# A decoder layer on one core: context loads issued by ScalarE, two queues at the start, set-up products spread out, the last two bases kept on chip

## What is computed

```python
x = x + attention(layernorm(x))          # 16 heads of 32; q, k, v and output weights of 512x512
x = x + cross(ctx, ctx, layernorm(x))    # one head of 512 over 750 context rows
h = layernorm(x)
scores = (h @ Wq.T @ Wr.T) @ (keys @ Wr.T).T / sqrt(48) + mask     # 2048 keys
top, idx = top_k(scores, 8)
agg = sum(softmax(top) * values[idx])                  # gather of 8 rows of 512
var = log1p(variance(h));  u = 0.5 * var / (mean over the whole input of var + 1e-6)
gate = sigmoid(g * clip(u + 2.5 * sigmoid(learned(h)), 0, 5) + gb)
x = x + (h + gate * agg)
```

## Time and profile before, and how it is read

| what | before |
|---|---|
| median of 3 runs | 2828.26 us |
| the profiled execution, its own time | 2849.81 us |
| its span, first to last instruction | 2847.7 us |
| TensorE busy | 2571.2 us, 90% of the span |
| VectorE busy | 2142.2 us, 75% |
| ScalarE busy | 1443.6 us, 51% |
| GpSimd busy | 694.1 us, 24% |
| moved by DMA | 360.72 MB |

### The profile page before, as it was taken

How to read it: one execution, slowest core, us unless ns; L and a number is a source line. 1 busy time by engine, 2 the same in 40 slices (tenths; PEclk the granted TensorE clock), 3 DMA queues, 4 the chain that set the end, 5 groups by cost and what they waited for, 6 DMA issues and landing times. The chain is left out here.

```text
span 2847.7 us, 56945 instructions
## 1 busy us (share of the span) xinstructions
PE 2571.2 (90%) x19090; PEld 2098.2 (74%) x19090; DVE 2142.2 (75%) x4203; ACT 1443.6 (51%) x4252; POOL 694.1 (24%) x652
## 2 busy tenths in 40 slices
PE   6699999999999999999999999999999999999720
PEld 3477788877887888778887888778787888778510
DVE  4446788888888888888887888888888888787641
ACT  2345545555555555555555555555555455555252
POOL 0000222222222222222222222222222222222344
PEclk8799999999999999999999999999999999999855
DMA  5212444444444444444444445444444444444888
GB/s 185 52 52 69 127 108 137 127 135 116 127 126 126 130 104 141 122 130 121 132 117 129 126 113 135 129 128 122 132 114 129 116 127 133 131 112 114 226 198 170
DMA packets 132519, 360.72 MB, mean 127 GB/s; under 512 B 21986, under 2 KB 26594, under 8 KB 124243
## 3 DMA queue, kind: packets, MB, share of 16 engines
q1 hardware_dynamic: 68468, 198.53, 24.0%
q0 software_dynamic: 64000, 161.52, 22.8%
HBM read 316.83 MB, written 43.15 MB: 126 GB/s over the span
## 5 line engine op out<-in xcount | busy, mean ns | idle before, releaser
L589 POOL DMA_INDIRECT vg<-in_L_ffn_aux_values,idx x512 | 501.9, 980 | 858.1 <-DVE agg L999 627.8
L660 ACT ACTIVATE pa<-psA,nmax 112x224 f32<-112x224 f32 x1024 | 443.7, 449 | 263.2 <-DVE nmax L891 152.5
L891 DVE TENSOR_REDUCE nmax<-psA 112x4 f32<-112x896 f32 x256 | 267.4, 1086 | 139.8 <-PE psA L1170 139.8
L1104 PE MATMUL psX<-big,gT 128*112 128x375 f32 x1024 | 333.4, 478 | 0.6 <-ACT gT L687 0.6
L999 DVE SCALAR_TENSOR_TENSOR agg<-vg,wt,agg 112x512 f32<-112x512 f32 x420 | 314.6, 749 | 9.6
L1104 PE MATMUL psX<-pT,cx 125*128 125x224 f32 x1536 | 299.1, 355 | 0.0
L1104 PEld LDWEIGHTS psX<-pT,cx 125*128 125x128 f32 x1536 | 288.0, 190 | 4.0 <-issue 0.3
L906 DVE TENSOR_TENSOR pa<-pa,rsum 112x896 f32<-112x896 f32 x256 | 279.6, 1092 | 8.9 <-DVE rsum L904 0.2
L1113 PE MATMUL psA<-ident,pa 112*112 112x112 f32 x2048 | 238.3, 265 | 42.5 <-DVE oT_lo L869 23.0
L1104 PEld LDWEIGHTS psX<-big,gT 128*112 128x112 f32 x1024 | 175.5, 176 | 125.7 <-issue 0.9
L1113 PEld LDWEIGHTS psA<-ident,pa 112*112 112x112 f32 x2048 | 202.3, 135 | 78.9 <-DVE pa L906 33.7
(11 more groups left out here) (217 smaller groups left out, 6033.5 us busy)
## 6 DMA issues: line engine op xcount, KB each, us to landing
big<-in_ctx_t SPq DMA_DIRECT2D x32, 1500.0 KB, 8.3
cx<-in_ctx SPq DMA_DIRECT2D x32, 1344.0 KB
xa<-in_x SPq DMA_DIRECT2D x64, 224.0 KB, 2.9
centered<-in_x_t SPq DMA_DIRECT2D x32, 448.0 KB
x<-in_x SPq DMA_DIRECT2D x32, 448.0 KB, 4.2
x<-in_L_attn_bff POOLq DMA_DIRECT2D x32, 448.0 KB
x<-cb_scratch POOLq DMA_DIRECT2D x32, 448.0 KB, 6.0
out<-x SPq DMA_DIRECT2D x32, 448.0 KB, 3.1
```

The lines of the kernel that those rows point to most:

```text
L589: pool.indirect_dma_start(vg[:, c % SLOTS, k, :], None, aux_values, bass.IndirectOffsetOnAxis(ap=idx[:, t, n:n + 1], axis=0))\
L660: last = nc.scalar.activation(pa[:, t, h, :], psA[0:R, h, t * S:(t + 1) * S], ACT.Exp, bias=nmax[:, k % 2, h, t:t + 1], accum_out=rsum[:, ...
L891: nc.vector.tensor_reduce(nmax[:, k % 2, h:h + 2, :], psA[0:R, h:h + 2, 0:T * S].rearrange("p h (t s) -> p h t s", t=T), AX_X, ALU.max, ne ...
L1104: last = nc.tensor.matmul(dst, stationary, moving, start=n == 0, stop=n == len(pairs) - 1)
```

## The change

Per-engine effect of the new `ORDER`: TensorE, ScalarE and VectorE do ("X", "prob", 1) right after ("F", "learn", 0), ahead of ("F", "score", 0) and ("A", "mix", 1). VectorE does ("G", "sum", 6) ahead of ("X", "mix", 0). GpSimd does ("R", "bias", 0) as the last step, behind ("F", "top", 1) with the first gathers. SP does ("N", "spread", 0) ahead of ("G", "sum", 2) and ("R", "load", 0) ahead of ("G", "sum", 7), and has no more step at ("X", "score"). The other swaps in `ORDER` are between steps of different engines.

`LAST` is another order of the same steps: ("X", "enter", 0, 31) stands ahead of ("G", "sum", 0, 29); the sums of 29 come earlier among the X steps; ("G", "sum", 3, 30) stands ahead of ("F", "route", 0, 31), and sums 4 and 5 of 30 follow close behind; only three scalings stand ahead of ("F", "turn", 0, 31) (there were five), and ("F", "top", 0, 31) and ("F", "top", 1, 31) stand ahead of more of the scalings. SP's loads stand in another order: 19 of them ahead of ("Z", "load", 25, 31), the first that needs ("X", "out", 1, 31), and the other nine directly behind it as far as SP is concerned.

```diff
-FIRST = (("W", "mean", 0), ("N", "norm", 0), ("N", "spread", 0), ("W", "split", 0), ("W", "mean", 1), ("N", "center", 0),
-         ("W", "split", 1), ("W", "mean", 2), ("W", "split", 2),
-         ("W", "keys", 0), ("W", "keys", 1), ("W", "keys", 2), ("W", "keys", 3))
-SETUP = {1: (("W", "route", 0), ("W", "m2", 0)),
-         2: (("W", "m2", 1), ("W", "m2", 2), ("W", "m2", 3), ("W", "router", 0), ("W", "wff", 0)),
-         7: (("W", "cb", 0), ("W", "m1", 0), ("W", "m1", 1)),
-         12: (("W", "m1", 2), ("W", "m1", 3), ("W", "gb", 0))}
+FIRST = (("N", "norm", 0), ("N", "spread", 0), ("W", "mean", 0), ("N", "center", 0), ("W", "split", 0),
+         ("W", "mean", 1), ("W", "mean", 2), ("W", "split", 1), ("W", "split", 2), ("W", "keys", 0),
+         ("W", "keys", 1),)
+SETUP = {1: (("W", "keys", 2),),
+         2: (("W", "keys", 3),),
+         3: (("W", "router", 0), ("W", "route", 0), ("W", "m2", 0),),
+         7: (("W", "m2", 1), ("W", "wff", 0), ("W", "m2", 2),),
+         10: (("W", "m2", 3), ("W", "cb", 0), ("W", "m1", 0),),
+         13: (("W", "m1", 1),),
+         14: (("W", "m1", 2),),
+         17: (("W", "m1", 3), ("W", "gb", 0),)}
...
-        DIRECT = B - 2
+        DIRECT, WHOLE = B - 3, B - 2
+        base = {WHOLE: base30, WHOLE + 1: x2}
...
-        kept = [pa[:, :, :, :].rearrange("p t h s -> p (t h s)"), paT[:, :, :, :].rearrange("p t h s -> p (t h s)")]
+        kept = [over_qk[:, :], pa[:, :, :, :].rearrange("p t h s -> p (t h s)"), paT[:, :, :, :].rearrange("p t h s -> p (t h s)")]
...
         @block.sync
...
-            sp.dma_start(staged[0], rows(attn_wq_t)).then_inc(weight_loaded[0], 16)
             load_x(0)
             sp.dma_start(flat(centered), row(x_t, 0)).then_inc(xt_loaded, 16)
-            sp.dma_start(staged[1], rows(attn_wk_t)).then_inc(weight_loaded[1], 16)
...
+            sp.dma_start(staged[0], rows(attn_wq_t)).then_inc(weight_loaded[0], 16)
...
-            def next_cxT(b, t):
...
-            def next_ctx(b, part):
-                if part == 0 or (isinstance(b, int) and b == B - 1):
-                    return
-                wait_full(sp, "X", FILL["X", "mix", 1], b)
-                if not (isinstance(b, int) and b + 3 >= B):
+            def next_rows(b, part):
+                if part == 1 and not (isinstance(b, int) and b + 3 >= B):
+                    wait_full(sp, "X", FILL["X", "mix", 1], b)
                     load_x(b + 3)
-                load_ctx(b + 1)
...
+            def store_whole(_, n):
+                if n >= WHOLE:
+                    sp.wait_ge(merged, n - WHOLE + 1)
+                    sp.dma_start(tiles(row(out, n)), late_tile[n]).then_inc(late_stored[LATE + n - DIRECT], 16)
+
             def store_base(b, _):
+                if isinstance(b, int) and b >= WHOLE:
+                    return
...
         @block.gpsimd
...
-                nc.gpsimd.tensor_tensor(x2[:, :, :], x2[:, :, :], xnf[:, :, :], ALU.add).then_inc(base_ready, 1)
+                dst = x2
+                if isinstance(b, int) and b >= WHOLE:
+                    dst = base[b]
+                    wait_full(pool, "A", FILL["A", "mix", NB - 1], B - 1)
+                nc.gpsimd.tensor_tensor(dst[:, :, :], x2[:, :, :], xnf[:, :, :], ALU.add).then_inc(base_ready, 1)
...
             def add_scaled(_, n):
+                if n >= WHOLE:
+                    return
...
         @block.scalar
+            act.dma_start(staged[1], rows(attn_wk_t)).then_inc(weight_loaded[1], 16)
+            act.dma_start(staged[2], rows(attn_wv_t)).then_inc(weight_loaded[2], 16)
+            act.dma_start(keysT, aux_keys_t).then_inc(keys_loaded, 16)
...
+            act.dma_start(x1[:, :, :], tiles(row(x, 0))).then_inc(xr_loaded, 16)
...
             def x_exp(b, t):
...
+                if t == 1 and not (isinstance(b, int) and b == B - 1):
+                    act.dma_start(big[:, :], row(ctx_t, b + 1)).then_inc(cxT_loaded, 16)
...
             def x_mixed(b, part):
...
                 nc.scalar.copy(uT[0][:, 2 * part:2 * part + 2, :], chunks("X", j)).then_inc(uT_hi, 1)
+                if part == 1 and not (isinstance(b, int) and b == B - 1):
+                    load_ctx(act, b + 1)
...
             def scale(_, n):
+                if n >= WHOLE:
+                    return
...
             def x_out(b, t):
...
-                    wait(dve, base_stored, 16 * b)
+                    if isinstance(b, int) and b == B - 1:
+                        dve.wait_ge(base_ready, b)
+                    else:
+                        wait(dve, base_stored, 16 * b)
...
+            def merge(_, n):
+                if n < WHOLE:
+                    return
+                dve.wait_ge(gate_ready, 1 + (n == B - 1))
+                dve.wait_ge(base_ready, n + 1)
+                dve.wait_ge(summed, CHUNKS * (n + 1))
+                for t in range(T):
+                    last = nc.vector.scalar_tensor_tensor(late_tile[n][:, t, :], late_tile[n][:, t, :], gate[:, T * n + t:T * n + t + 1],
+                                                          base[n][:, t, :], ALU.mult, ALU.add)
+                last.then_inc(merged, 1)
```

More of the change, by code:

```diff
@@ L340, in row, with load_ctx, rows @@
             return t[b, :, :] if isinstance(b, int) else t[bass.ds(b, 1), :, :].rearrange("a s d -> (a s) d")
+        def load_ctx(eng, b):
+            src = row(ctx, b).rearrange("(p j) d -> p j d", j=KC)
+            for part in (slice(0, R), slice(R, KP)):
+                eng.dma_start(cxv[part], src[part]).then_inc(ctx_loaded, 16)
+        def rows(w):
+            return w.rearrange("(c p) d -> p c d", p=P)
         def over_rows(v):
@@ L405, in _ @@
         def _(sp):
-            def rows(w):
-                return w.rearrange("(c p) d -> p c d", p=P)
             def load_x(b):
@@ L463, in first_ctx @@
                 sp.wait_ge(setup_drained, FILLED)
[L464 to L476 removed]
+                load_ctx(sp, 0)
+            def next_rows(b, part):
+                if part == 1 and not (isinstance(b, int) and b + 3 >= B):
+                    wait_full(sp, "X", FILL["X", "mix", 1], b)
                     load_x(b + 3)
[L478 removed]
             def store_moments(b, _):
@@ L540, in load_agg @@
                 sp.dma_start(late[k], tiles(row(agg_dram, n))).then_inc(late_loaded[k], 16)
-            pipeline(sp, {("Z", "load"): load_agg, ("W", "split"): after_split, ("W", "keys"): after_keys,
+            pipeline(sp, {("Z", "load"): load_agg, ("Z", "scale"): store_whole, ("W", "split"): after_split, ("W", "keys"): after_keys,
                           ("W", "cb"): first_cxT, ("W", "gb"): first_ctx,
-                          ("X", "score"): next_cxT, ("X", "mix"): next_ctx, ("N", "norm"): store_moments,
+                          ("X", "mix"): next_rows, ("N", "norm"): store_moments,
                           ("N", "spread"): spread_moments, ("N", "center"): next_xt, ("X", "enter"): entered, ("R", "load"): next_xr,
@@ L547, in _ @@
                           ("G", "sum"): store_agg})
-            for k in range(LATE + 2):
-                sp.wait_ge(late_stored[k], 16 * (1 + (k < DIRECT - LATE)))
+            for k in range(LATE + B - DIRECT):
+                if k < DIRECT or k >= LATE:
+                    sp.wait_ge(late_stored[k], 16 * (1 + (k < DIRECT - LATE)))
         @block.gpsimd
@@ L613, in _, with small @@
         def _(act):
+            def small(dst, src):
+                act.dma_start(dst, src).then_inc(small_loaded, 16)
+            act.dma_start(staged[1], rows(attn_wk_t)).then_inc(weight_loaded[1], 16)
+            act.dma_start(staged[2], rows(attn_wv_t)).then_inc(weight_loaded[2], 16)
+            act.dma_start(keysT, aux_keys_t).then_inc(keys_loaded, 16)
+            act.dma_start(rwT[:, 0:RD], router_w_t).then_inc(look_up_loaded, 16)
+            act.dma_start(rwT[:, LO:RS], router_w_t).then_inc(look_up_loaded, 16)
+            act.dma_start(qw, q_proj_w).then_inc(look_up_loaded, 16)
+            act.dma_start(unc1T[:, :, :], unc_w1_t.rearrange("(c p) f -> p c f", p=P)).then_inc(look_up_loaded, 16)
+            act.dma_start(woT, rows(x_wo_t)).then_inc(wo_loaded, 16)
+            with nc.allow_non_contiguous_dma(reason="bias columns, once"):
+                small(bvc[:, :], x_bv.rearrange("(c p) -> p c", p=P))
+                small(bqc[:, :], x_bq.rearrange("(c p) -> p c", p=P))
+                small(b1c[:, :], unc_b1.rearrange("(p a) -> p a", a=1))
+                small(w2c[:, :], unc_w2.rearrange("a p -> p a"))
+            small(cb[:, :], x_bo.partition_broadcast(R))
+            small(b2c[:, :], unc_b2.partition_broadcast(R))
+            small(gwc[:, :], gate_w1.partition_broadcast(R))
+            small(gbc[:, :], gate_bias.partition_broadcast(R))
+            act.dma_start(x1[:, :, :], tiles(row(x, 0))).then_inc(xr_loaded, 16)
             def copy_out(s, j, b, dst, src):
```

40 lines of the change are left out of this document (8 added, 32 removed), and 67 rows, old and new, of tables (LAST, ORDER).

## The result

The changed kernel has a median of 2799.98 us over 4 runs (2798.26 to 2803.3); the kernel before, run beside it, 2826.62 us (2824.95 to 2828.69). The ratio is 0.9907, 95% interval [0.989, 0.9924]: 26.6 us less. The forecast was 2781: the direction is right and the time lies inside the range of 2760 to 2807, but 19 of the 45 to 47 us of gain did not come.

A forecast was written before the change was run, and what follows sets the result against it. TensorE was taken to bound the loop, DMA engines the end. Start 30, loop 3 and end 14 us made 47 less, taken from the runs' median of 2828: 2781 us, range 2760 to 2807.

The forecast's parts named there:

- One term of the loop: Loop: ScalarE's three new load issues per batch run beside its arithmetic and cost 0; upper end 22 us.
- issues on ScalarE's path: Rival, 20%: the new load issues hold up ScalarE's arithmetic in the loop, 22 us back, 2803 us.
- The start: Set-up and batch 0: batch 1 begins 30 us earlier, from 7.8 net before "qk", 16 of waits, 6 of clock.
- 16 + 6 less the two keys: Batch 0: 16 us of TensorE waits and 6 us of clock gained, less two moved "keys" products, 2 us.
- near 1: Sign of being right, batch 0: TensorE's granted clock near 1, where the mean was 0.80.
- late moments: Rival, 15%: at the start, the moments' store and return wait for the DMA backlog; 12 us lost, 2793 us.
- the loop's period grows by 0.3 us or more: Sign of being wrong, in the loop, whose batches were expected to stay at 80 us.
- The end: Last stretch, bound by the DMA engines: four changes together 14 us less, with ends of 4 and 22.
- (c): End: ten loads in SP's order no longer stand behind the base of batch 31; 4 us less.
- (d): End: fewer accumulations ahead of a gather and earlier searches of batch 31 shrink idle DMA time; 5 us less.
- (a): End: sums of batch 29 and bases of 30 and 31 skip moves through DRAM; 3.6 us less.
- (b): End: accumulations 30 and 31 become plain stores, 1.8 us for 2.5 each; 1.4 us less.

The follow-up runs named there:

- the kernel before, once more: The kernel before the change, with no edit, run and profiled a second time: 2830.06 us, ratio 1.0005.

## Why the prediction was right or wrong

**One term of the loop, put at nothing, was 16.5 us.** With `cx` not in ScalarE's way the change gives 44.1 us, 45.6 and 43.5 in three versions; I forecast 47. With it, 26.6. So the step that failed is this one: "If it runs beside the arithmetic, the first lies beside 1.1 us of exponentials just handed over, and the second ends at 1333.2, before the copy that matters ... I take **0**". The first half is right: `big`'s 0.36 us lie beside 1.12 us of exponentials, and putting it back on SP changes nothing that the runs can tell. The second half is wrong twice. What is handed over at `uT_hi` is one cast, behind whose start the copies could begin at 0.42 us, and the two issues keep the sequencer for 0.97 (0.06 + 0.91). And the copy that matters is the last of four: all four follow one another without a gap (1.83 us, x4), where the earlier trace rows show two pairs and 0.32 idle between them. That idle time is the long execution's wait on `pa`, passed on to ScalarE in every one of its batches. This is TensorE's row there, and the copies of the kernel before, once more:

```profile
1333.65 0.97 PE L1113 MATMUL psA<-ident,pa 112*112 112x112 f32 x8 [0.31 <-DVE pa L906]
```

```profile
449.29 1.84 ACT L616 COPY paT<-psA 112x448 f32<-112x448 f32 x4
```

The four copies take 1.84 us at 1561.81 and 2040.86 too, with no such slack. The cost is 0.64 us a batch by the periods, 16.5 us by the medians of the changed kernel (21.2 on the old order), inside the prediction's upper end of 22. It was the rival *issues on ScalarE's path*, with 20%: near in size, and wrong in its place, since half of its 22 was put on `big`, which costs none, and 0.39 us a batch on `cx`, which costs 0.64. (0.88 less 0.14 and 0.32 is 0.42, and not the 0.39 of the prediction; the upper end would be 23.) The Trainium skill, page Perfetto Trace Analysis, section DVE / Act Engine Instruction, has the sequencer push an instruction and go on; the trace agrees for a single issue behind two exponentials, and at `uT_hi` shows what the rule leaves to the reader: the sequencer goes on to the issues, and the copies behind them start only 0.11 us after the issues end.

**The start.** 30 us were forecast, 19.0 came. Batch 0 itself is right: it takes 82.9 us (40.38 to 123.28) for 102.5, 19.6 less, and 16 + 6 less the two keys is 20. TensorE's busy time in it fell from 79.98 to 75.63 and the rest from 24.0 to 8.4 us, 15.6 for my 16, and of the wait on `oT_lo` 3.1 us are left, as forecast. The granted clock is 0.90 for 0.80; "near 1", one of the signs, it is not. What failed is "SP issues four loads, x first, so the store can go when the moments are there: some 9 to 10 us, since x no longer waits for wq", and behind it "I put 2 us less here: `centered` at 18". The moments were ready at 12.8, 0.8 us later than before and not sooner. In all the kernels here they are ready between 11.9 and 13.0 us, and latest where seven or more other loads go out on ScalarE's queue beside x. Store and return then took 13.4 us, not 8.0. ScalarE, put at "free at about 19 to 20", was held by its issues until 24.69. `centered` at 26.22 is 8.2 late, "qk" 7.7; from `centered` on, my 14.7 us to "qk" were 14.2. The order of the set-up alone gives 18.1 of the 19.0, so the two queues, for which with split 0 behind the centring I had 9.8 us, are worth 0.9 by the totals; batch 1 starts 3.9 us sooner with them, and the intervals leave room for either. That is the mechanism of the rival *late moments*, at two thirds of its size: "qk" at 40.4 between the forecast's 32.7 and its 44.7. The Trainium skill, page DMA: Bandwidth & Descriptors, section Issuing engines are not separate DMA queues, says that a second issuer saves issue time and no more; by that rule the 8.5 us of issuing were to be had, and the trace shows less, since a store that goes 7.8 us sooner (12.79 for 20.55) meets the backlog and is 3.4 us longer under way (13.4 for 10.0). With the small loads, Wo and the residual's x out of its way it takes 9.7.

**The loop otherwise.** The waits on `nx` went, worth 3 by my sum, and the new order as a whole gave 4.4; the reason given first, that SP is rid of two waits, is not the one, since with the old order and the loads on ScalarE 2.7 us of them stay. One sign of being wrong, "the loop's period grows by 0.3 us or more", came: 0.44 against a usual execution of the kernel before. Against the profiled one, whose loop was too long, it could not be seen.

**The end.** 14 forecast, 16.6 measured. (c) and (d), the order, 9 us: 8.0 to 8.8. (a) and (b), the bytes, 5 us: about 8. VectorE's waits for the gathers of batch 30 into `pa`, 15.98 us at the longest, are at most 3.71 in the changed kernel and 6.08 with the new `LAST` alone, so that is the order's doing. Those of batch 31 into `paT` hardly change: 31.1 us in all for 33.6, and 9.28 for 9.48 on the last.

The parts measured alone sum to 40.0 us without ScalarE's issues, together they give 43.5 to 45.6. Each is known to 2.5 to 4 us, and I leave open whether these few us are more than that.

**The range.** That the time fell inside it is in part luck. The range took in each rival by itself and left out any two together, and two came: 11 us of the start and 16.5 of the loop, which from 2781 make 2808.5, beyond its end of 2807. The end and the new order gave 4 us more than forecast, and the few us of the last paragraph did the rest.

## What to carry to other kernels

A DMA issue moved to a computing engine cost here what it delayed the next instruction that somebody waited for (1.08 us behind the cast's start in place of 0.42), and nothing where enough arithmetic had been handed over ahead of it or where it stood behind the last such instruction. A profiled execution that is far above the median of the runs (here 21.5 us, 0.8 a batch) can have waits that the others have not, and so slack behind them: the 0.3 us a batch that were read from this one are half of the 0.64 in question. At the start, ask what each transfer shares the DMA engines with rather than who issues it; what is small and not needed soon goes behind the round trip that everything waits for, and work whose inputs are there goes into that wait.

## What the hardware showed that I had not expected

The same load can hold its issuer for very different times. `bqc`, a bias column, took 6.24 us on ScalarE's sequencer at 11.19, with the DMA engines at 1.06, and 0.51 us on SP's at 20.02, with them at 0.39 in 20:21; Wo took 5.53 and 0.46. That a queue was full, as the prediction says of the issue of 4.16 us, no view shows; the share of the engines is what the windows give. In the changed kernel ScalarE was held until 24.69, 1.5 us before `centered` set the pace.

The store of 224 moments and the load behind it took 12.2 to 13.4 us beside the first loads, 9.7 with the small ones, Wo and the residual's x out of the way. And Wq, 1 MB, landed 17.8 us after its issue as the fourth load of SP, with 17 on the other queue, and 7.4 us after it as the first of ScalarE (issued at 0.77), with 5 other first loads beside it in place of 20.
